# A four-layer graph network on one core: the decoder's output bias moves from DVE to TensorE

## The reference

```python
z = relu(gcn_conv(z, edge_index, W_enc2, b_enc2, n))
z = relu(z @ W_dec1 + b_dec1)
x_hat = z @ W_dec2 + b_dec2
...
x = x + x_hat
```

## Time and profile before

| | us |
|---|---|
| median of 3 runs | 7803.85 |
| lowest and highest run | 7795.47, 7820.31 |
| the profiled execution | 7778.81 |
| its span in the profile | 7777.1 |
| PE busy in the span | 3451.5 (44%) |
| DVE busy | 5027.6 (65%) |
| ACT busy | 2878.4 (37%) |
| POOL busy | 4996.3 (64%) |

### The profile page before, as it was taken

The page is one execution under the profiler, slowest core; times in us unless marked ns, Lnnn a source line. Parts: engine busy times, 40 slices in busy tenths (PEclk is TensorE's granted clock), DMA queues, the critical chain, the costliest instruction groups (busy, mean ns, idle before and its releaser), DMA issues. The chain is left out here.

```text
span 7777.1 us, 107713 instructions
## 1 busy us (share of the span) xinstructions
PE 3451.5 (44%) x16871; PEld 2563.0 (33%) x16871; DVE 5027.6 (65%) x20181; ACT 2878.4 (37%) x6928; POOL 4996.3 (64%) x4625
## 2 busy tenths in 40 slices
PE   7201555555566788884000767700288333333000
PEld 1000333333456666664000555500266222222000
DVE  7767555555677888887776777622377255555654
ACT  0574000000577333333554666600133155555222
POOL 0002888888544677776665777277788677777577
PEclk9655656656788899997555888855699655555555
DMA  8897232333799333334666999822499333333343
GB/s 225 302 357 234 40 41 41 41 41 41 206 290 295 96 92 92 91 91 113 177 176 182 369 366 362 276 52 52 141 340 344 113 103 103 103 103 103 109 138 116
DMA packets 1124316, 1274.72 MB, mean 164 GB/s; under 512 B 220879, under 2 KB 933433, under 8 KB 1113734
## 3 DMA queue, kind: packets, MB, share of 16 engines
q1 hardware_dynamic: 924340, 976.28, 38.7%
q0 software_dynamic: 199904, 297.70, 16.4%
HBM read 680.81 MB, written 620.27 MB: 167 GB/s over the span
## 5 line engine op out<-in xcount | busy, mean ns | idle before, releaser
L655 POOL DMA_INDIRECT dense<-t_xs,ends x784 | 785.7, 1002 | 358.8 <-issue 183.1
L483 POOL DMA_INDIRECT g<-t_src,ends x398 | 401.6, 1009 | 772.0 <-DVE keyr L517 651.0
L1746 PE MATMUL ps<-dense,w 128*128 128x256 f32 x3136 | 730.3, 386 | 180.8 <-DVE dense L1457 150.2
L501 POOL DMA_INDIRECT t_acc<-tot,sidx x392 | 638.7, 1629 | 147.4 <-issue 130.0
L1746 PEld LDWEIGHTS ps<-dense,w 128*128 128x128 f32 x3136 | 580.9, 190 | 298.3 <-DVE dense L1457 188.3
L560 PE MATMUL ps<-ident,keyr 128*128 128x128 f32 x394 | 118.1, 398 | 1053.3 <-DVE seq L530 608.6
L741 ACT ACTIVATE estd<-emv,epsc 128x2 f32<-128x2 f32 (+1 forms) x588 | 174.1, 296 | 1027.9 <-DVE emv L724 1027.9
L1457 DVE SCALAR_TENSOR_TENSOR dense<-xT 128x256 f32<-128x256 f32 x1568 | 544.8, 420 | 2.8 <-ACT xT L1918 2.6
L655 POOL DMA_INDIRECT dense<-t_y,ends x392 | 373.1, 952 | 242.8 <-DVE ends L1550 155.4
L710 ACT ACTIVATE tot<-ps 128x256 f32<-128x256 f32 x196 | 75.1, 383 | 1224.0 <-PE ps L580 1224.0
L630 POOL DMA_INDIRECT t_yacc<-dense,gq x392 | 442.3, 1128 | 117.8 <-issue 112.8
(11 more groups left out here) (307 smaller groups left out, 12135.0 us busy)
## 6 DMA issues: line engine op xcount, KB each, us to landing
dense<-t_xs SPq DMA_DIRECT2D x78, 1320.0 KB
dense<-in_x SPq DMA_DIRECT2D x156, 640.0 KB
t_xs<-dense SPq DMA_DIRECT2D x98, 528.0 KB, 7.6
t_xs<-hb SPq DMA_DIRECT2D x78, 660.0 KB
t_sum<-dense SPq DMA_DIRECT2D x98, 512.0 KB
t_src<-dense SPq DMA_DIRECT2D x78, 640.0 KB
t_acc<-dense SPq DMA_DIRECT2D x78, 640.0 KB
dense<-t_acc SPq DMA_DIRECT2D x78, 640.0 KB
```

Source lines behind the costliest of these rows:

```text
L483: gp.indirect_dma_start(rows[:, p.k, c, :], None, table, bass.IndirectOffsetOnAxis(ap=gidx[:, p.k, c:c + 1], axis=0)) \
L501: gp.indirect_dma_start(target, bass.IndirectOffsetOnAxis(ap=sidx[:, p.k, c:c + 1], axis=0), t_out[:, p.k, c, :], None, compute_op=ALU.add ...
L655: gp.indirect_dma_start(rows[:, p.k, c, :], None, table, bass.IndirectOffsetOnAxis(ap=gidx[:, p.k, c:c + 1], axis=0)) \
L1746: i = nc.tensor.matmul(ps[:, o:o + 2 * P], w1[:, k, :], xm[:, p.w, k, :], start=(k == 0), stop=(k == R - 1))
```

## The change

The bias is no longer added to x on DVE. For each of the ten j, PE first multiplies one row of ones (stationary, 1 partition by 128 columns; 16 columns in the short block) with the first row of bd2b (moving, 128 columns) and starts the accumulator with it; the product with wd2s is added to that. `dec_bias` and its semaphore xb go, and `dec_x3` waits for the load of x itself.

```diff
-        L3 = phase("node", NB + 1, "sc own scal tr trc d1 d1c d2 xb x3",
+        L3 = phase("node", NB + 1, "sc own scal tr trc d1 d1c d2 x3",
...
-            def dec_bias(r, u, p):
-                v.wait_ge(L3["ld"][u].sem, L3["ld"][u].after(r * 16 + 16))
-                nc.vector.tensor_tensor(xin[u][0:p], xin[u][0:p], bd2b[0:p, :].rearrange("p (a f) -> p a f", a=1)
-                                        .to_broadcast([p, K, D]), ALU.add).then_inc(L3["xb"].sem, 1)
-
             def dec_x3(r, u, p):
...
                 v.wait_ge(L3["d2"].sem, L3["d2"].after(b + 1))
-                v.wait_ge(L3["xb"].sem, L3["xb"].after(b + 1))
+                v.wait_ge(L3["ld"][u].sem, L3["ld"][u].after(r * 16 + 16))
...
-            node_loop_back(v, (dec_x3, 3), (dec_bias, 2), (dec_scale, 0))
+            node_loop_back(v, (dec_x3, 3), (dec_scale, 0))
...
                 for j in range(K):
-                    i = nc.tensor.matmul(ps[0:p, DC + j * P:DC + (j + 1) * P], fT[u][:, j, 0:p], wd2s[:, :],
-                                         start=True, stop=True)
+                    o = DC + j * P
+                    nc.tensor.matmul(ps[0:p, o:o + P], ones[0:1, 0:p], bd2b[0:1, :], start=True, stop=False)
+                    i = nc.tensor.matmul(ps[0:p, o:o + P], fT[u][:, j, 0:p], wd2s[:, :], start=False, stop=True)
                 i.then_inc(L3["d2"].sem, 1)
```

## The result

The changed kernel took 8551.56 us (median of 4 runs, 8515.45 to 8583.48), the kernel before 7803.41 beside it: a ratio of **1.0954, 95% interval 1.09 to 1.1009**. The direction was as forecast, the size was not: +748 us where +326 us was forecast, and the time lies above the range.

The account below looks back on a forecast made before the run. No engine bounds the whole program; in the decoder stage POOL's last blocks leave TensorE 135.8 us of slack. Adding 2.24 + 3.61 = 5.85 us a block over 79 blocks gave +326 us, 8130 us; range 7840 to 8300.

Parts of the forecast that it names:

- What bounds the stage: Decoder stage: POOL's writes hold back the last blocks; without them TensorE would end at 6060.8 us instead of 6196.57.
- The slack of 1.72 us a block: Decoder stage: 135.8 us over 79 blocks; added TensorE time up to 1.72 us a block stays hidden under POOL.
- The first term: dec_out on TensorE: ten one-row products, 20 records at 0.112 us, add 2.24 us a block.
- The second term: dec_out on TensorE: 19 changes of stationary shape a block at 0.19 us each add 3.61 us.
- the period of 11.93 us at a clock near 1.00: Decoder stage: one block takes 6.08 us now plus 5.85 us added, with TensorE's clock staying up.
- rival (c): Decoder stage: TensorE's granted clock falls; 8280 us at 0.85, near 9000 at half throughout; chance 0.11.
- the prediction's own sign: Decoder stage: a granted TensorE clock under 0.9 would mean that the clock does not stay up.
- A: Decoder stage: TensorE time the change adds to each block, forecast at 5.85 us.
- Removing the addition on DVE "buys nothing": Decoder stage: dropping 79 additions of 1482 ns saves no time, since DVE is outside the TensorE chain.
- rival (d): Decoder stage: added products stay hidden under POOL, whose scatters may shorten beside lighter DMA queues; 7770 to 7804 us; chance 0.05.
- The waits: Decoder stage: SP's waits on POOL vanish; dec_x3's new wait for the load of x costs nothing, its dec_out wait being later.

Follow-up runs that it names:

- e1_identity: Changed kernel with the ten one-row bias products replaced by identity (128 rows) times the spread bias; 7827.11 us, 1.0037 of the kernel before.
- e6_half_precision_pair: Changed kernel with the bias as two float16 rows, added by three full-shape products a block, one a bank; 7777.61 us, 0.9967 of the kernel before.
- e2_bank: Changed kernel with three one-row bias products a block, each over a whole accumulator bank, in place of ten; 8172.87 us, 1.0483 of the kernel before.
- e7_bank64: Changed kernel with three bias products a block over whole banks, 64 stationary rows (63 zero) in place of one; 7896.38 us, 1.0124 of the kernel before.
- e5_rows64: Changed kernel with 64 stationary rows (63 zero) in place of one in each of the ten bias products; 8402.77 us, 1.0765 of the kernel before.
- e8_three: Changed kernel with the one-row product only for the first three of ten j, the rest without bias; 7844.51 us, 1.0052 of the kernel before.

## Why the prediction was right in its direction and wrong in its size

- **What bounds the stage** was right. With 2.24 us a block the stage was to end at 6237.8, and that of e1_identity ended at 6241.60. With 0.52 us (e6_half_precision_pair) POOL still held the last blocks back. The slack of 1.72 us a block stands. In time e1_identity took +27 us where +41 was worked out, because the profiled execution of the kernel before, from which the slack was read, was some 20 us faster than that kernel's median.
- **The first term**, 2.24 us for the products, was measured at 2.24 for products of 128 rows (e1_identity). For one row the dec_out of e2_bank at the full clock, 5.45 us, less 2.25 for its own products and 5 x 0.19 for the switches, leaves 2.25.
- **The second term**, 0.19 us a switch, was measured at about 0.19, in both directions. At the full clock a dec_out of the changed kernel would be 10 x 0.83 = 8.3 us, and with 64 rows one was 8.24; "about 8.3" was forecast.
- **The step that failed** is the one in the second term that takes its price from stretches at a clock of 1.00 and then multiplies it by 19 switches a block for the whole stage, that is, the period of 11.93 us at a clock near 1.00. One switch after a dense stretch shows the price of a switch but not what a stretch of switches does to the clock. Here the clock fell to a mean of 0.67, and the period became 17.1 us. This is rival (c), by the prediction's own sign (a clock under 0.9). Its price holds too: by it 11 us of work at a clock of 0.67 grow by 11 / 0.67 - 11 = 5.4 us a block, and some 4.95 were measured. But it got 0.11 against 0.60, on the argument that TensorE's idle gap stays under 1 us a block. That gap did stay under 1 us (0.87 or 0.95, in e1_identity as in the changed kernel), and the clock fell all the same when one-row products alternated with full ones (0.67), and stayed up with the same number of full-shape ones (1.00). So the granted clock does not follow idle gaps alone.
- **The size, split.** The stage ended at 6930.98, so A was (6930.98 - 6060.8) / 79 = 11.0 us a block. Of that 8.3 - 2.25 = 6.05 us are the change at the full clock, 79 x 6.05 - 135.8 = 342 us; the other 4.95 us, 391 us in all, are the clock: slower pairs in a part of dec_out and a dec_hidden of 3.4 to 4.5 us in place of 2.33.
- **Removing the addition on DVE "buys nothing"** was wrong by a little: alone it is worth 34 us, and POOL's scatters, longer beside it (1.15 us on average in place of 1.06), explain about 20 of them, as much as the two profiled executions differ by (7778.81 and 7758.85). The prediction had a gain for POOL in rival (d), but put it down to the load on the DMA queues, which is nearly the same in both runs (0.95 and 0.97).
- **The waits** went as forecast: SP no longer waits for POOL, and dec_x3 waits for dec_out only.

What stays open is the exact condition under which the clock falls. The runs show what bears on it (rows spanned: e2_bank against e7_bank64; switches, with the longer dec_out that they make: e5_rows64 against e7_bank64; the amount of one-row work at five switches: e8_three against e2_bank), no more.

## What to carry to other kernels

A product of one row was as dear on TensorE here as one of 128 rows with as many moving columns (2.25 and 2.24 us for 1280), and dearer between full ones: each change between an operand of 65 or 128 rows and one of 64 or fewer cost about 0.19 us, and ten such products a block brought the clock down to 1.2 GHz for a good part of each block. To put a bias into an accumulator, use a stationary operand of the full shape, one product for a whole bank, and where the precision allows it a 16-bit pair of rows. And when a price is read from a trace at the full clock, ask whether the new loop will keep that clock; a run with the new mix of shapes tells it, the share of busy time does not.

## What was not expected of the hardware

TensorE can be busy 94.6% of the time by its records and be granted a clock of 0.67, and busy 90% at a clock of 1.00 (e7_bank64); its share of busy time did not show the clock. A float16 product and float32 products can follow each other into one accumulator without a visible gap (0.22 us from the start of a float16 record of 512 columns to the next). And POOL's scatters that began while DVE added two operands from SBUF (line 1574) took 1.53 us on average, where 0.97 is usual.
